# The row order of block 4's queries and keys: part by part, or dimension by dimension

## What is computed

```
x = x + L1_xattn(layernorm(x), ctx, ctx, mask)

q = split_heads(query @ Wq.T + bq)          # 16 heads of 16 dimensions
k = split_heads(key @ Wk.T + bk)
scores = einsum('bhtd,bhsd->bhts', q, k) / sqrt(16)
scores = where(mask, scores, -inf)
attn   = softmax(scores)
out    = einsum('bhts,bhsd->bhtd', attn, v) @ Wo.T + bo
```

## Time and profile before

| | us |
|---|---|
| median of 3 runs | 506.22 (499.56 to 510.32) |
| the profiled execution: its time | 508.15 |
| its span | 506.4 |
| TensorE busy | 429.4 (85%) |
| VectorE busy | 265.5 (52%) |
| ScalarE busy | 163.3 (32%) |
| GpSimd busy | 130.1 (26%) |
| mean granted TensorE clock | 0.885 of full speed |
| chain that ended last | TensorE 65%, VectorE 11%, DMA 10%, GpSimd 6% |

### The profile page before, as it was taken

How to read it: one execution, slowest core, us unless ns; L and a number is a source line. 1 busy time by engine, 2 the same in 40 slices (tenths; PEclk the granted TensorE clock), 3 DMA queues, 4 the chain that set the end, 5 groups by cost and what they waited for, 6 DMA issues and landing times.

```text
span 506.4 us, 7332 instructions
## 1 busy us (share of the span) xinstructions
PE 429.4 (85%) x2920; PEld 280.8 (55%) x2920; DVE 265.5 (52%) x481; ACT 163.3 (32%) x334; POOL 130.1 (26%) x174
## 2 busy tenths in 40 slices
PE   2999986959999974997999999961979969979986
PEld 1556743535667754874555557640346646646654
DVE  5056676992146520236675998651953634643423
ACT  0440430004531231322537424021143534523731
POOL 4620075327441066056100000006003213300100
PEclk9999998969999886999999999995575795975989
DMA  8991020001116963320000029976175256320002
GB/s 242 363 246 37 1 63 27 0 0 45 44 45 192 370 262 113 84 71 20 1 2 0 0 37 134 126 128 90 37 111 75 38 71 91 62 31 2 3 1 65
DMA packets 30616, 42.17 MB, mean 83 GB/s; under 512 B 4330, under 2 KB 27286, under 8 KB 30186
## 3 DMA queue, kind: packets, MB, share of 16 engines
q1 hardware_dynamic: 28279, 35.95, 28.6%
q0 software_dynamic: 2304, 5.76, 7.1%
HBM read 33.00 MB, written 8.98 MB: 83 GB/s over the span
## 4 chain that ended last, share of the span: by engine, by line
PE 65%; DVE 11%; DMA 10%; POOL 6%; ACT 4%; issue 3%; SPq 1%; ACTq 0%; DVEq 0%; POOLq 0%
PE banks L1193 13%; PE banks L1259 6%; PE banks L951 5%; PE banks L1299 5%; PE banks L1286 5%; DMA RC<-NT 4%; PE banks L1006 4%; PE banks L980 3%; PE banks L1227 3%; PE banks L940 2%; DVE RA L449 2%; PE banks L1031 2%; PE banks L1112 2%; PE banks L1130 2%; DMA RC<-q_parts 2%
## 5 line engine op out<-in xcount | busy, mean ns | idle before, releaser
L1604 DVE TENSOR_REDUCE NM<-banks 100x2 f32<-100x722 f32 x64 | 57.2, 906 | 63.2 <-PE banks L1259 62.4
L1193 PE MATMUL banks<-XT,RBG 128*128 128x400 f32 x192 | 65.0, 500 | 2.1 <-ACT XT L744 2.1
L1193 PEld LDWEIGHTS banks<-XT,RBG 128*128 128x128 f32 x192 | 36.3, 190 | 29.8 <-issue 1.2
L899 ACT ACTIVATE CT<-banks 128x400 f32<-128x400 f32 (+1 forms) x72 | 35.9, 504 | 41.9 <-PE banks L1286 40.8
L598 POOL TENSOR_TENSOR rstd<-ve,mhalf 100x4 f32<-100x4 f32 x12 | 12.5, 1040 | 140.0 <-DVE ve L1359 140.0
L744 ACT ACTIVATE XT<-banks 128x800 f32<-128x800 f32 x14 | 11.6, 838 | 98.6 <-PE banks L940 98.6
L1259 PE MATMUL banks<-RBG,RC 97*100 97x361 bf16 x64 | 23.1, 464 | 13.6 <-DMA RC<-q_parts 12.2
L940 PE MATMUL banks<-identf,XN 100*128 100x100 f32 x112 | 17.1, 309 | 17.5 <-DVE XN L1364 10.0
L1299 PE MATMUL banks<-CT,RV 128*17 128x100 f32 (+1 forms) x576 | 28.4, 293 | 0.0
L1286 PE MATMUL banks<-RC,RBG 100*128 100x100 bf16 (+1 forms) x192 | 21.7, 254 | 7.6 <-DMA RC<-NT 7.6
L1286 PEld LDWEIGHTS banks<-RC,RBG 100*128 100x128 bf16 (+1 forms) x192 | 18.3, 140 | 15.4 <-DMA RC<-NT 8.7
(11 more groups left out here) (228 smaller groups left out, 832.8 us busy)
## 6 DMA issues: line engine op xcount, KB each, us to landing
RA<-in_L_ffn_W SPq DMA_DIRECT2D x2, 2048.0 KB, 11.8
k_parts<-RA SPq DMA_DIRECT2D x18, 180.5 KB, 3.4
RBG<-in_L_attn_W_aiv SPq DMA_DIRECT2D x1, 3072.0 KB, 16.1
CT<-in_ctx_t SPq DMA_DIRECT2D x2, 1444.0 KB, 11.4
RC<-q_parts SPq DMA_DIRECT2D x12, 200.0 KB, 6.7
RBG<-k_parts SPq DMA_DIRECT2D x12, 180.5 KB, 8.8
RA<-k_parts SPq DMA_DIRECT2D x12, 180.5 KB, 9.1
RBG<-k_parts POOLq DMA_DIRECT2D x12, 180.5 KB, 6.5
```

Of the source, the lines that this page charges most:

```text
L899: sc.activation(P4[slot][0:n, g * HG * T:(g + 1) * HG * T], PS[4 + w % 2][0:n, 0:HG * T], ACT.Exp).then_inc(st_exp, 1)
L1193: ins = mm(PS[2 * aiv_pair(i) + g][:, 0:GC], WA[:, k, c:c + P], XT[:, k, GC * g:GC * g + GC], start=(k == 0), stop=(k == KT - 1))
L1604: v.tensor_reduce(NM[:, b % 2, 2 * i:2 * i + 2], PP[w % 2][0:T, :, 0:S], AX.X, ALU.max, negate=True).then_inc(mx_out, 1)
```

## The change

The six loads keep their number, size, source, order and issuer. What changes is where the 16 dimensions of load r go: from partitions 16r to 16r + 15, side by side, to partitions r, r + 6, r + 12, ..., r + 90. Rows 96 to 99 stay, and so do all matmuls: queries and keys are reordered alike.

```
-                    queue.dma_start(QS[DK * r:DK * r + DK, g].rearrange("d (k h) n -> d k (h n)", h=HK),
+                    queue.dma_start(QS[r:ROW_MASK:len(PARTS), g].rearrange("d (k h) n -> d k (h n)", h=HK),
                                     q_parts[qp, g].rearrange("k (d h) n -> d k (h n)", h=HK)
                                     ).then_inc(qs_ld[g], 16)
...
-                queue.dma_start(KS[s][DK * r:DK * r + DK].rearrange("d (k h) s -> d k (h s)", h=HK),
+                queue.dma_start(KS[s][r:ROW_MASK:len(PARTS)].rearrange("d (k h) s -> d k (h s)", h=HK),
                                 k_parts[kp, b].rearrange("k (d h) s -> d k (h s)", h=HK)
                                 ).then_inc(ks_ld[b], 16)
```

## The result

The kernel after takes 471.0 us (median of 4 runs, 468.59 to 478.37) against 506.63 (499.56 to 510.32): a ratio of 0.932, 95% interval 0.919 to 0.946, so 35.6 us or 7% less. Run again later beside other kernels it took 472.2 us (ratio 0.941, interval 0.933 to 0.950). The forecast was 469 us, range 461 to 491.

What follows compares the result with a forecast made beforehand. Bound: TensorE in block 4, stopped by slow query and key loads and then at half clock. First queries 6.7, waits 11.7 and half clock 20.2 us sum to 38.6 off 508.15: 469 us, own range 462 to 478, wider range 461 to 491.

Steps and rivals of the forecast that it cites:

- the sum: Whole kernel: 6.7 + 11.7 + 20.2 = 38.6 us saved from the profiled 508.15.
- First queries: Start of block 4: faster query loads and an earlier store bring the first maximum to 345.5 from 352.18, saving 6.7 us.
- The rate: Block 4's key and query loads: 312 GB/s, three quarters of 416, where 118 to 136 were measured.
- The earlier store: Before block 4's first queries: the first query store lands 1.2 us earlier, no longer behind draining key loads.
- Waits and half clock, sequences 1, 3 and 5: Block 4: TensorE's three waits for the maxima's small loads go, 11.7 us, and the half clock behind them, 20.2 us.
- not in 2 to 4: Sign in the profile after: the small loads of the maxima land in 2 to 4 us.
- The source as the limit: Rival: reading DRAM scratch limits the key and query loads, so no effect, 506 us; chance 9%.
- The slower rival: Rival: a DMA engine carrying one dimension stops at the same few rows; 100 GB/s gives 520 us; chance 5%.
- the even sequences' small loads gain nothing: Block 4: these small loads land 2.0 us before their score, so speeding up the keys ahead of them gains nothing.
- rate only partly better: Rival: 150 to 180 GB/s leaves waits of some 2 us and the clock falls; about 495 us; chance 4%.

Runs made afterwards that it cites:

- the single stop of 4.35 us put back into sequence 3: The kernel after with the keys of sequence 5 alone in the old row order; 484.6 us, ratio to before 0.968.
- the loads alone: No reference computation; SyncE alone issues sets of six loads from input or scratch in several row orders, each set waited for; rates read, 112 to 270 GB/s.
- two experiments: Kernel after with all keys in the old order, 494.5 us; and with new order only for queries and keys of sequences 5 and 7, 487.6 us.
- with 213 GB/s the runs: The kernel after with loads r and r + 1 sharing 32 neighbouring rows, each taking every second one; median 479.3 us, 469.59 to 487.73.

## Why the prediction was right, step by step

The profiled executions differ by 508.15 - 468.59 = 39.6 us; the sum had said 38.6. The medians differ by 35.6, as the profiled execution of before lies 1.5 us above its median and that of after 2.4 below. The parts are therefore checked in the traces.

**First queries.** Predicted 6.7 us, first maximum at 345.5. It starts at 346.19 instead of 352.18: 6.0, of which 0.4 arose before block 4. From the first load's issue to the first maximum it takes 346.19 - 339.03 = 7.2 us, not 6.2. The rate was mis-sized, 269 GB/s where I took 312, and I had left SyncE's issues at 0.42 us. The earlier store came nearly as said: from the first store's issue to the first load's it takes 339.03 - 335.89 = 3.1 us instead of 4.2, so 1.0 us less where I took 1.2.

**Waits and half clock, sequences 1, 3 and 5.** Predicted 11.7 + 20.2 = 31.9 us. From the first maximum to the end of the fifth output projection the kernel before takes 466.16 - 352.18 = 114.0 us, the kernel after 428.34 - 346.19 = 82.2: 31.8. Piece by piece (to the first, third and fifth projection) it is 10.7, 11.0 and 10.1 us, where I had 10.7, 10.8 and 10.4: the mechanism, and not only the sum. The clock is part of this by experiment, not by argument: the single stop of 4.35 us put back into sequence 3 lengthened this stretch by about 10 us. The small loads land 3.6 to 4.6 us after their issue in sequences 2 to 5, not in 2 to 4; that is why 0.54 us of waiting is left.

**The rest.** 39.6 - 6.0 - 31.8 = 1.8 us lies behind the fifth projection. I had not counted it. Before, the last output projection ran at half clock, 1.95 us; after, it takes 1.11. But it can't be credited to the change: the second profiled execution of the kernel after has partly half clock there too, and takes 43.1 us from the fifth projection to its end, against 40.3 in the first and 42.0 before. So the total came within 1 us of the sum partly by luck: 1.1 us too much at the first queries, 2.2 us that the sum doesn't hold.

**The rate.** The source as the limit is refuted by the loads alone (137 and 133 GB/s side by side, 264 and 264 with step six). The slower rival, engines held up at six neighbouring rows, isn't seen: it needed about 100 GB/s, and step six moved 221 to 269 in the windows above. What it is in sixteen neighbouring rows that slows a load, these runs don't show, only by how much.

**What was wrong in the working.** First, "the even sequences' small loads gain nothing". It holds only with half clock behind the stops of the odd ones. With their keys in the old order and full clock they stopped TensorE by 3.1 to 3.7 us each (two experiments); the forecast came out since their keys were sped up as well, which its sum valued at nothing. That is luck. Second, I let the clock fall behind waits of some 2 us and more and not behind those of 1 us; the trace had shown only stops of 3.8 us and more. It fell behind 1.20 and 0.97 us too, and did not behind 1.03 and 0.94. So the case "rate only partly better" has no single time. I gave it 495 us for 150 to 180 GB/s, which no run has; with 213 GB/s the runs lie between 470 and 488, according to the clock they were granted.

## What to carry to other kernels

When DMA engines are busy but move a third of what they move elsewhere with runs of the same length (118 to 136 GB/s against 402 to 416 here), look at which partitions the transfer writes; a contraction's rows may be permuted freely, so the layout that spreads each load cost the matmuls nothing here (at full clock, before and after, four of line 1286, of 100 columns, take 0.34 to 0.35 us, and two of line 1259, of 361 columns, 0.51). Spread each single load, and not only the set (137 against 264 GB/s over the same 96 rows). A short stop of TensorE in a stretch that TensorE bounds is to be priced with the half clock behind it (4.35 us cost about 10 here), and a load that is hidden under a slow stretch is not hidden once that stretch is fast. When whole executions differ by 5 us for reasons of their own, read a change's price between two marks in its own stretch.

## What was not expected of the hardware

- Small transfers issued on SyncE's queue landed 3.6 to 4.6 us after issue behind GpSimd's key loads at 221 to 247 GB/s, 7.5 to 8.1 us behind them at 124 (sequences 3 and 5), and 1.7 us alone: the wait follows the time the large loads take, across queues. The runs show these times, and not why a queue waits for the other.
- All 128 rows with step eight (233 GB/s) are slower than 106 rows with step seven (270 GB/s) and 96 with step six (264).
- Stops of about 1 us are followed by half clock in some cases (0.97 and 1.20 us) and not in others (0.94 and 1.03).
